# Fewer semaphore waits ahead of the matmuls of the feed-forward stage

## The reference

```python
def _L0_ffn_ref(x, W, b, lora_A, lora_B, gate_w, gate_b):      # D = O = 2048
    base = x_flat @ W.T + b
    logits = x_flat @ gate_w.T + gate_b                        # 8 experts
    topk_logits, topk_idx = jax.lax.top_k(logits, 2)
    gates = jax.nn.softmax(topk_logits, axis=-1)
    xA = jnp.einsum('nd,erd->ner', x_flat, lora_A)             # 8 experts x rank 16 = 128
    delta_all = jnp.einsum('ner,eor->neo', xA, lora_B)
    ...
    out = base + lora_update
x = x + _L0_attn_ref(_layernorm(x), Wq, Wk, Wv, Wo)
x = x + _L0_ffn_ref(_layernorm(x), W, b, lora_A, lora_B, gate_w, gate_b)
```

## Time and profile before

| | us |
|---|---|
| median of 2 runs | 4899.37 (4856.69 to 4942.06) |
| the profiled execution, its own time | 4513.26 |
| its span on the slowest core (core 5) | 4511.7 |
| spans of the eight cores | 4484.7 to 4511.7 |
| mean granted TensorE clock of the eight cores | 0.836 to 0.845 |

### The profile page before, as it was taken

How to read it: one execution, slowest core, us unless ns; L and a number is a source line. 1 busy time by engine, 2 the same in 40 slices (tenths; PEclk the granted TensorE clock), 3 DMA queues, 4 the chain that set the end, 5 groups by cost and what they waited for, 6 DMA issues and landing times. The chain is left out here.

```text
span 4511.7 us, 68251 instructions; the slowest of 8 cores (4484.7 to 4511.7 us)
## 1 busy us (share of the span) xinstructions
PE 3562.5 (79%) x18452; PEld 1701.8 (38%) x18452; DVE 1648.1 (37%) x4528; ACT 1138.9 (25%) x2606; POOL 543.3 (12%) x1106
## 2 busy tenths in 40 slices
PE   2787888888888696788827878888888886957888
PEld 1333434434443242344413334334344432423444
DVE  1334345445445111233313343454454451112333
ACT  5224233224224100111152242332242241001111
POOL 3101001001001101011031010010010011010110
PEclk9887878888898797788857868888879887977888
DMA  4110110110110746312141101101101107562111
GB/s 154 27 26 18 21 23 15 20 24 15 20 24 1 158 159 131 85 76 76 69 156 28 27 16 19 24 15 20 24 15 20 24 1 159 159 134 82 75 75 76
DMA packets 55548, 258.56 MB, mean 57 GB/s; under 512 B 13720, under 2 KB 13984, under 8 KB 34720
## 3 DMA queue, kind: packets, MB, share of 16 engines
q0 software_dynamic: 36464, 119.66, 13.3%
q1 hardware_dynamic: 14128, 100.98, 6.8%
q10 hardware_dynamic: 4608, 33.56, 2.1%
HBM read 273.15 MB, written 67.11 MB: 75 GB/s over the span
## 5 line engine op out<-in xcount | busy, mean ns | idle before, releaser
L822 ACT ACTIVATE prT<-dg,cstt 128x128 bf16<-128x128 f32 (+1 forms) x576 | 216.5, 386 | 1851.0 <-POOL dg L794 1306.1
L783 DVE TENSOR_SCALAR sp<-ps 128x512 f32<-128x512 f32 (+3 forms) x1104 | 623.5, 592 | 83.8 <-ACT prT L836 26.6
L1081 PE MATMUL cb<-wf,cT 128*128 128x512 bf16 x2048 | 514.7, 414 | 96.9 <-DMA wf<-wf 74.8
L776 PE MATMUL ps<-QT,KT 128*128 128x512 bf16 (+3 forms) x1104 | 480.8, 477 | 126.8 <-DVE sp L783 82.3
L847 ACT ACTIVATE prT<-sp,cstt 128x128 bf16<-128x128 f32 (+2 forms) x1368 | 577.0, 487 | 0.1
L714 PE MATMUL pz<-va,prT 128*128 128x129 bf16 x3652 | 375.0, 258 | 248.9 <-ACT prT L847 95.8
L406 PE MATMUL bp<-wo,zTt 128*128 128x512 bf16 x2048 | 469.9, 394 | 72.6 <-DMA wo<-wo 72.6
L620 PE MATMUL pp<-xnT,wv 128*128 128x512 bf16 x2048 | 467.7, 391 | 0.0
L620 PE MATMUL pp<-xnT,wq 128*128 128x512 bf16 x2048 | 447.2, 379 | 0.0
L620 PE MATMUL pp<-xnT,wk 128*128 128x512 bf16 x2048 | 447.2, 379 | 0.0
L714 PEld LDWEIGHTS pz<-va,prT 128*128 128x128 bf16 x3652 | 273.9, 113 | 412.2 <-issue 412.0
(11 more groups left out here) (105 smaller groups left out, 2431.7 us busy)
## 6 DMA issues: line engine op xcount, KB each, us to landing
prT<-x SPq DMA_DIRECT2D x32, 1024.0 KB, 5.1
bx<-x SPq DMA_DIRECT2D x32, 1024.0 KB, 6.6
x2d<-b POOLq DMA_DIRECT2D x32, 1024.0 KB, 8.6
c<-x2d ACTq DMA_DIRECT2D x32, 1024.0 KB, 4.9
out<-co SPq DMA_DIRECT2D x32, 1024.0 KB, 3.9
wv<-wv POOLq DMA_DIRECT2D x32, 512.0 KB, 6.1
wq<-wq POOLq DMA_DIRECT2D x32, 512.0 KB, 5.9
wk<-wk POOLq DMA_DIRECT2D x32, 512.0 KB, 5.6
```

The costliest lines, as they stand in the source:

```text
L776: lambda e, c=c, q0=q0, n=n, bank=bank: e.matmul(psc[bank][:, 0:n], KT[:, c * 128:(c + 1) * 128], QT[:, q0 * 128: q0 * 128 + n], start=Tru ...
L783: lambda e, n=n, bank=bank, buf=buf: e.tensor_scalar(spanb[buf][:, 0:n], psc[bank][:, 0:n], 1024.0, -1024.0, ALU.min, ALU.max),
L822: soff=soff: e.activation(probsT[:, pslot:pslot + min(ncols, 128)], diagb[:, soff:soff + min(ncols, 128)] if ncols == 64 else diagb[:, 0:128],
L1081: lambda e, bi=bi, dc=dc, og=og, bk=bk: e.matmul(b["pb"][bk][:, :], b["xnT2"][bi][:, dc * 128:(dc + 1) * 128], b["wfT"][:, dc * D + og * 5 ...
```

## The change

TensorE executes its stream in order, so a wait on a semaphore that an earlier instruction of the same stream has already waited for is met at once. The change leaves out such waits in stage C: in steps 2 and 3 only the first matmul of each four keeps its wait on `trs`, in step 4 only the first of each four of `base_chunks(0)`, and `base_chunks(1)` to `(3)` keep none on `trs`. The waits on weights (`s_wg`) and on banks (`gl_evac`, `xa_evac`, `base_evac`) stay. No operation, tile or transfer is added, removed or moved.

```diff
         for dc in range(NDC):                     # step 2 (L942)
-            w = [(s_dve, trs[dc // 4])]
+            w = [(s_dve, trs[dc // 4])] if dc % 4 == 0 else []
...
         for dc in range(NDC):                     # step 3 (L965)
-            w = [(s_dve, trs[dc // 4])]
+            w = [(s_dve, trs[dc // 4])] if dc % 4 == 0 else []
...
             for dc in range(NDC):                 # base_chunks (L1081)
-                w = [(s_dve, trs[dc // 4])]
+                w = ([(s_dve, trs[dc // 4])]
+                     if (og == 0 and dc % 4 == 0) else [])
```

## The result

| | before | changed kernel |
|---|---|---|
| median, us | 4690.9 (10 runs, 4515.19 to 4942.06) | 4533.82 (11 runs, 4459.93 to 4901.03) |
| ratio | 1 | 0.9864, 95% interval 0.9817 to 0.991 |
| span of the profiled execution | 4511.7 | 4464.8 |
| mean granted clock of the cores | 0.836 to 0.845 | 0.840 to 0.847 |

What follows compares the result with a forecast made beforehand. TensorE's stream was taken as the bound. Gate and LoRA waits, with a guess for the clock, gave 1.25 us a tile, times 30 tiles 37.5 us; ratio 0.9917 of 4899.4 gave 4859 us, range 4795 to 4930.

Steps and rivals of the forecast that it cites:

- the scale that turned a ratio into microseconds: Whole kernel: ratio 0.9917 applied to 4899.4 us, the median of two runs, giving 4859 us.
- The bound: Stage C: TensorE's stream is the path, PE busy 89%, one tile every 27.31 us.
- The 60 waits at L1081: Ahead of 512-column base matmuls: removal saves nothing, 216 ns start to start with or without a wait.
- the copies of `cT` do not take the waits' place: Gate: last two copies end at 4399.99, before the fourth group of matmuls would be reached at 4400.19.
- 12 x 70 and 12 x 19 ns: Gate saves 0.84 us, LoRA 0.23 at half clock or 0.84 at full; together 1.07 to 1.68 us a tile.
- The clock's part: Shifted clock falls leave 0.54, 1.07 to 1.68, or 3.1 us saved a tile; 1.25 us was taken.
- third rival: Second clock fall behind the gate's round trip, second run 8.75 us; 1.1 us a tile slower, 4935 us; chance 0.10.
- the prediction's own signs of being wrong: Stage C: gate matmuls staying near 127 ns, period staying 27.3 us, or second runs of 8.7 us becoming common.
- the full clock for about 84% of the time: Profile's clock line: read as TensorE having the full clock for that share of the time.
- First rival: Period stays 27.3 us: clock takes all back, or waits don't make the 127 ns; 4899 us, chance 0.17.
- Second rival: Shorter gate and LoRA stretch, clock no longer falls: 3.1 us a tile, 93 us, 4798 us; chance 0.07.
- What is late next: VectorE's gate chain, ahead of L1096: 0.2 us left if the covering run shrinks from 8.47 to 7.07 us.

Runs made afterwards that it cites:

- a1_dense: Kernel before, only the 60 waits a tile ahead of the 512-column matmuls of base_chunks removed; ratio 1.0003, tile 27.51 us.
- b4_pipe: Stage C rearranged against the changed kernel: four base banks, next tile's transposes and gate round trip among the base matmuls, fewer waits; ratio to before 0.9507.
- c4_gate: Kernel before, only the gate's 12 waits a tile removed; ratio 0.9984, tile 27.24 us.
- b3_double: Kernel before with every wait in gate and LoRA put down twice, 32 more a tile; ratio 1.0256, tile 31.14 us.
- b1_fill: Changed kernel with useless 128-column matmuls in the transposes' stall and the gate's round trip; ratio to before 0.9749, tile 23.75 us.
- c1_dose: Changed kernel with 6 of LoRA's 12 removed waits put back; ratio to before 0.9908, tile 26.03 us.
- a4_both: Kernel before, the gate's and LoRA's 24 waits removed, those of base_chunks kept; no ratio, tile 25.65 us.

## Why the prediction was right and wrong

Two steps failed: the scale that turned a ratio into microseconds, and the size of what the waits cost in gate and LoRA. The mechanism, fewer waits in the issue of short matmuls with a part going back to the clock, was right.

- **The bound.** TensorE's stream sets the tile: right. Every microsecond of difference was found in it.
- **The 60 waits at L1081 are worth nothing:** right (a1_dense, 1.0003). That the copies of `cT` do not take the waits' place: wrong. Gate matmuls are so much faster that the last two groups do wait for them. In the changed kernel the last two copies are these, in the timeline of DVE:

```profile
4385.27 0.76 DVE L924 COPY cT<-ptc 128x512 bf16<-128x512 bf16 x2 [0.31 <-PE ptc L916]
```

They end at 4386.03; the third group of gate matmuls starts at 4385.84 and the fourth at 4386.17, each over 0.25 us behind the matmul before it. Without that wait, in b4_pipe, 16 take 0.48 us, with it 0.98.
- **The size of the term "12 x 70 and 12 x 19 ns" failed.** It said 1.07 to 1.68 us a tile; the rows show 4.72 - 2.83 = 1.9 to 4.72 - 2.04 = 2.7. Of these the gate is 1.05 us, where 0.84 was forecast, and LoRA up to the first big matmul 0.76 at half clock and 1.52 at full, where 0.23 and 0.84 were (the remaining 0.1 us is at the gate's bias matmul). It was wrong in three ways. First, I priced a gate matmul without a wait at L714's 57 ns. b4_pipe shows 0.48 / 16 = 30 ns, and single starts lie 25 ns apart. L714's row is of another shape, 129 columns, and the rows of before have no matmul of 8 columns without a wait. Second, I left the kept waits at 127 ns each. With one wait in four all 16 LoRA matmuls follow at 0.90 / 16 = 56 ns at the full clock, as in b4_pipe without any on `trs` (4018.84 to 4019.74), and at 104 ns at half. So each of the 16 was worth 70 or 23 ns, not each of 12. Third, the sum had nothing for the end of LoRA. Before, the first big matmul starts 0.51 us behind the last of LoRA (4401.60 + 15 x 0.127 = 4403.51, and 4404.02). Now it is 0.10 us (4411.24 + 15 x 0.104 = 4412.80, and 4412.90), and the 0.4 us are the rest of LoRA's gain. No run takes this end apart, and its cause stays open.
- **The clock's part** I put in as a guess between its cases. The case that happened is a mixture that the prediction did not price: the long fall became short, and in 120 of 224 tiles the third rival's second fall came, with the very 8.75 us run of the earlier trace rows. That was one of the prediction's own signs of being wrong. The third rival was to decide from every second tile on; it didn't, since the saving was 2.3 us and not 1.07. Of these 2.26 us on average 1.71 are left. That 1.25 us were forecast and 1.71 came is an error in the saving, partly covered by the guess for the clock. And "the full clock for about 84% of the time" was misread: 0.84 is the mean, and with levels of 1.00 and 0.50 it means full clock for some two thirds of the time (on core 5 it was at half for 1472 us of 4512).
- **First rival (a lock, nothing comes of it):** wrong for the change, and exactly right for either half of it (27.24 and 27.29 us). The reason that I gave against it, 127 against 57 ns, was true and no argument: c4_gate has the faster matmuls and no gain. Its other reading, that the waits aren't what makes 127 ns, is out by b3_double: with a second wait the starts of short matmuls lie 232 ns apart in place of 126.
- **Second rival (the clock stays up):** not in the change, but b1_fill brought it about: 23.75 us a tile.
- **What is late next,** VectorE's gate chain with 0.2 us left: the right chain. In b1_fill, with the clock up, it is late by 0.26 us.
- **The time failed by its scale.** 4859 us was 0.9917 times 4899.4, the median of two runs, though the prediction saw that it lay 8.6% above the profiled execution; its range of 4795 to 4930 allowed only the 0.9% by which these two runs lay from their median. The ten runs of the kernel before go from 4515 to 4942 us, and the changed kernel's median is 4533.82. The scale was wrong by more than the whole effect. Scaled on the profiled execution the forecast was 4475.8 us, and 4466.33 was measured: 37.5 us less were forecast and 46.9 came. Within 2% was right.

What stays open: why c1_dose and the changed kernel settle in just the sequences of tiles that they do. I have shown that the falls hang on the stalls and that the second fall eats the gain of each half, not a rule that gives the sequence for any saving.

## What to carry to other kernels

Where a TensorE stage has stalls in it, look at the granted clock over one period before pricing an edit: a saving of 1 us can vanish nearly whole into a second fall of the clock (c4_gate: 1.17 us saved up to the first big matmul, a tile of 27.24 us in place of 27.40), and two such savings together can pay more than their sum (0.1 us each alone, 1.7 in a4_both). Here the waits that were already met were worth removing ahead of the matmuls of 8 and 128 columns only (126 ns from start to start with them, 25 and 56 without at the full clock; 216 at 512 columns either way), and one in four could stay. The larger prize is to fill the stalls, best with the work of the next tile: the rearranged stage was 3.6% faster than the change here.

## What was not expected of the hardware

- A met wait ahead of a short matmul makes 126 ns from start to start, two make 232, and this is the same at both levels of the clock; ahead of 512 columns, or at one 128-column matmul in four, it cannot be seen (216 and 56 ns at the full clock).
- Matmuls of 8 columns with a weight load of 128 columns each follow at 25 ns (b4_pipe), less than half the 56 ns of LoRA's matmuls, which have the same weight load: the load doesn't set that pace of 56.
- 40 useless matmuls in each tile make the changed kernel faster by 1.2%, since the clock stays at its upper level (b1_fill: no fall in the 224 tiles).
